# A one-column memset on VectorE replaced by a one-column tensor_tensor, 192 times, in an attention and mixture-of-experts kernel on one core

## The reference

```python
x = L0_attn_x                                   # (4, 512, 256)
xn = layernorm(x)
# attention: 16 query heads, 4 key/value heads, head size 128, rotary embedding with xpos scale
q, k, v = xn @ Wq, xn @ Wk, xn @ Wv
scores = einsum('bhqd,bhkd->bhqk', q, k) / sqrt(128)
attn = softmax(where(causal, scores, -inf))
s = (attn @ v) @ Wo
# feed-forward: 16 experts of 176, the best 2 of each token, and a shared expert of 352
g = silu(moe(xn) + shared(xn))
x = x + s * g
```

## Time and profile before

| | us |
|---|---|
| median of 3 runs | 763.02 |
| lowest, highest | 761.98, 763.47 |
| the profiled execution, its own time | 763.02 |
| its span, first to last instruction | 761.2 |

### The profile page before, as it was taken

One profiled execution on the slowest core, in us unless ns is written; L12 is line 12 of the kernel. 1 busy time (PEld: TensorE's weight loads), 2 busy tenths in 40 slices (PEclk: granted clock), 3 DMA queues, 4 the chain that ended last, 5 costly groups with the idle time before them and its releaser, 6 DMA issues.

```text
span 761.2 us, 17791 instructions
## 1 busy us (share of the span) xinstructions
PE 669.6 (88%) x5090; PEld 470.8 (62%) x5091; DVE 635.3 (83%) x1756; ACT 457.4 (60%) x1269; POOL 514.8 (68%) x543
## 2 busy tenths in 40 slices
PE   3678876789999999999999999999985879999983
PEld 1256544456667666676666766667664558778751
DVE  6988999988999899998999989999875975454477
ACT  3684645446756567575675766757664756666642
POOL 4676656648678886888868888688844734444474
PEclk9999999989999999999999999999998999999997
DMA  9490000500000000000000000000004864444562
GB/s 297 158 318 19 1 1 0 135 23 15 1 14 7 7 14 0 14 7 7 14 0 14 14 0 14 0 14 14 0 15 131 233 102 131 124 132 133 194 249 83
DMA packets 45747, 50.40 MB, mean 66 GB/s; under 512 B 9906, under 2 KB 39058, under 8 KB 45714
## 3 DMA queue, kind: packets, MB, share of 16 engines
q1 hardware_dynamic: 41602, 39.44, 17.6%
q0 software_dynamic: 3840, 10.52, 3.9%
q10 hardware_dynamic: 272, 0.02, 0.0%
HBM read 31.01 MB, written 18.96 MB: 66 GB/s over the span
## 4 chain that ended last, share of the span: by engine, by line
POOL 36%; DVE 21%; issue 19%; PE 15%; ACT 5%; DMA 3%; POOLq 0%; SPq 0%; DVEq 0%; ACTq 0%
POOL arena L520 15%; POOL arena L507 9%; POOL arena L514 8%; PE bank L1455 6%; PE bank L1495 5%; POOL xs_dram L537 4%; DVE arena L375 3%; ACT arena L660 2%; DVE arena L1026 2%; PE bank L1464 2%; DMA arena<-x 1%; DVE arena L1000 1%; DVE arena L1001 1%; DVE s_sb L1174 1%; PE bank L1475 1%
## 5 line engine op out<-in xcount | busy, mean ns | idle before, releaser
L520 POOL TENSOR_TENSOR arena<-arena,rinv 128x128 f32<-128x128 f32 (+3 forms) x256 | 176.4, 720 | 119.4 <-DVE rinv L1020 119.4
L660 ACT ACTIVATE arena<-bank,nmax 128x512 f32<-128x512 f32 (+3 forms) x256 | 132.5, 533 | 69.8 <-DVE nmax L1014 69.8
L1014 DVE CUSTOM_DVE_ANT_0 bank<-bank,mask_b 128x512 f32<-128x512 f32 (+3 forms) x256 | 118.1, 516 | 11.9 <-issue 11.9
L1328 PE MATMUL bank<-arena 128*128 128x512 f16 (+7 forms) x768 | 119.6, 307 | 3.4 <-DVE arena L1032 3.2
L1268 PE MATMUL bank<-xnT_hi,arena 128*128 (+1 forms) x320 | 111.0, 389 | 11.2 <-DVE arena L1001 6.2
L1299 PE MATMUL bank<-arena 128*128 128x512 f16 (+7 forms) x768 | 116.9, 303 | 3.2 <-POOL arena L514 3.1
L668 ACT CAST arena<-bank 128x512 f16<-128x512 f32 (+1 forms) x192 | 93.2, 522 | 42.0 <-PE bank L1312 40.4
L1312 PE MATMUL bank<-ident_f,arena 128*128 128x128 f32 x640 | 92.6, 276 | 25.0 <-DVE arena L1026 18.3
L1026 DVE TENSOR_TENSOR arena<-bank,arena 128x512 bf16<-128x512 f32 (+1 forms) x192 | 109.0, 596 | 3.0 <-ACT arena L668 0.9
L507 POOL TENSOR_TENSOR arena<-arena 128x512 f32<-128x512 f32 x77 | 99.7, 1295 | 7.1 <-DVE arena L1001 6.8
L1312 PEld LDWEIGHTS bank<-ident_f,arena 128*128 128x128 f32 x640 | 74.0, 142 | 37.8 <-DVE arena L1026 22.4
(11 more groups left out here) (147 smaller groups left out, 1259.8 us busy)
## 6 DMA issues: line engine op xcount, KB each, us to landing
xs_dram<-s_sb SPq DMA_DIRECT2D x4, 1548.0 KB, 14.3
arena<-xs_dram SPq DMA_DIRECT2D x48, 128.0 KB
stage<-w_gate_up SPq DMA_DIRECT2D x16, 352.0 KB
arena<-ys_dram SPq DMA_DIRECT2D x8, 512.0 KB, 6.6
stage<-w_down SPq DMA_DIRECT2D x16, 176.0 KB
stage<-wq SPq DMA_DIRECT2D x4, 512.0 KB, 8.7
stage<-wo SPq DMA_DIRECT2D x4, 512.0 KB, 7.3
stage<-x SPq DMA_DIRECT2D x1, 2048.0 KB
```

The costliest lines, as they stand in the source:

```text
L520: ins = pool.tensor_tensor(pr, pr, rinv[:, par, qt:qt + 1].to_broadcast([P, (qt + 1) * P]), ALU.mult)
L660: ins = act.activation(probs[par][:, P_AT[qt]:P_AT[qt] + n], score_bank[u][:, col:col + n], ACT.Exp, scale=-1.0, bias=nmax[:, par, qt:qt + ...
L1014: ins = dve.tensor_tensor_reduce(score_bank[u][:, col:col + n], score_bank[u][:, col:col + n], mask_b[:, S - n:S], -1.0, 3e38, ALU.add, AL ...
L1328: ins = pe.matmul(o_bank[:, kt * P:S], v_s[a][:, kt * DH:(kt + 1) * DH], pT[j % 2][m][:, PT_AT[kt]:PT_AT[kt] + n_q], start=(kt == 0 and n ...
```

## The change

A tile `one` of one float32 column is added, and POOL sets it to 1.0 once, behind its first memset. In `row_max` the memset of one column of `waited` becomes a tensor_tensor that multiplies `one` by `one` into the same column. It carries the same wait and stands at the same place, three times for each head. Since the new memset raises `zeroed` too, the counts that are waited for go up by one, and DVE waits for it once, before the first `row_max`. No other instruction is added, removed or moved on any engine.

```diff
+        one = sb("one", [P, 1], F32)
...
             pool.memset(s_sb[:], 0.0).then_inc(zeroed, 1)
+            pool.memset(one[:], 1.0).then_inc(zeroed, 1)
             pool.memset(ones_b[:], 1.0).then_inc(zeroed, 1)
...
                     dve.wait_ge(scores, h * 3 + u + 1)
-                    dve.memset(waited[:, par, u:u + 1], 0.0)
+                    dve.tensor_tensor(waited[:, par, u:u + 1], one[:], one[:], ALU.mult)
                     for qt, col in unit:
...
             dve.wait_ge(mask_zero, 1)
+            dve.wait_ge(zeroed, 2)
             row_max(0, 0)
...
-            dve.wait_ge(zeroed, 3)
+            dve.wait_ge(zeroed, 4)
...
-                pe.wait_ge(zeroed, 2)
+                pe.wait_ge(zeroed, 3)
```

## The result

| | before | after |
|---|---|---|
| median, us | 762.87 | 798.02 |
| lowest, highest | 761.98, 763.47 | 794.78, 802.08 |
| span of the profiled execution | 761.2 | 794.4 |

The ratio is 1.045, with a 95% interval of 1.0418 to 1.0482: 35 us slower, where +58 was forecast. First the page's busy line, to be read beside the earlier trace rows, then the stretch of the earlier trace rows.

What follows compares the result with a forecast made beforehand. PE bounds the loop at 31.0 us a round; with the waits DVE becomes the bound at 35.1. +43 us in 12 loop rounds and +15 elsewhere, +58 on 763.0, gives 821 us, range 788 to 859.

Steps and rivals of the forecast that it cites:

- The mechanism: In `row_max`, the two-SBUF-input instruction waits for the end of POOL's tensor_tensor in flight; 86%, centre 821 us.
- rivals 1 and 2: At the changed instruction: first, no blocking, 771 us, 8%; second, not slower, hidden like the memset, 763 us, 5%.
- the signs: Rows of `waited` up to 1.3 us, mean 0.5 to 0.6; loop round 35 us; DVE over 93%, PE under 92%.
- Rival 3: POOL's instructions are delayed by DVE as well: at most 0.1 us each, 12 a round; chance included in the 86%.
- The mean wait: Per changed instruction in the loop, arriving at a random moment of POOL's work: 0.37 us, thinned to 0.33.
- The instruction itself: Each changed instruction's own fixed cost on DVE's queue, without waiting: 0.08 us.
- Together: Wait plus own cost on DVE per loop round: 12 x (0.33 + 0.08) = 4.9 us more, giving 33.9 us.
- The idle time that is kept: In a loop round DVE keeps half of its 2.5 us idle time, 1.2 us, making the round 35.1 us.
- Outside the loop: The 48 instructions in prologue and rounds 0, 1, 2 and 15: 48 x 0.41 x 0.75 = +15 us.
- The lower bound: Waits line up within a head, 0.25 us each plus 0.04: +1.0 to +2.2 us a round, 789 to 803 us.
- that DVE waits for one POOL instruction only: A blocked DVE instruction waits only for the POOL instruction in flight and gets through before the next queued one.
- The clock: PE, less busy at 88%, might get 0.9 of its clock, 34.4 us a round: nothing added, reason for upper half.

Runs made afterwards that it cites:

- e1: Changed kernel with the one-column tensor_tensor replaced by a one-column reciprocal of `one` (one SBUF input instead of two): 766.73 us.
- e2: Changed kernel with the tensor_tensor reading two different one-column tiles instead of the same tile twice: 795.41 us.
- e8: Changed kernel with the tensor_tensor only ahead of the first unit of each head, memsets ahead of the other two: 790.85 us.
- e9: Changed kernel with a memset ahead of the first unit of each head, tensor_tensors ahead of the second and third: 769.78 us.
- e7: Changed kernel with two one-column tensor_tensors in each place, the second into a tile of its own: 811.29 us.
- e11: Changed kernel with the tensor_tensor replaced by a tensor_copy, `one` and the target two columns wide: 795.80 us.

## Why the prediction came out as it did

**The mechanism was right.** The wide spread of the rows, their ends with POOL's, DVE as the bound of the loop, the unchanged end: all as written. One input less takes nearly all of the loss away (e1), and the same tile twice makes no difference (e2), so rivals 1 and 2 fall. What the Trainium skill, page "SBUF — State Buffer", section "Who interferes with whom", infers of descriptor generation, which I gave 5 us, holds as well: the row at 391.97 passes beside an indirect DMA. Four of the signs had the right direction and the wrong size: the mean row is 0.38 us for 0.5 to 0.6, the longest 2.04 for 1.3, the round 33.6 for 35, and PE is busy 93% where under 92% was said.

**Rival 3 had shown itself in one row before.** POOL's 1.44 us at 140.43 followed a DVE instruction of 256 columns and two SBUF inputs:

```profile
138.44 2.30 DVE L953 TENSOR_TENSOR compare<-held,steps 128x256 f32<-128x256 f32 x1
```

It ends at 140.74, POOL's instruction ahead at 140.46, and the next one is 0.17 us longer than the usual 1.27. With one column nothing of the kind is left (446.9 and 446.7 us of POOL's tensor_tensors, before and after).

**The size was too large, 58 for 35 us.** Per loop round I had +3.6 us and it was +2.1. By the steps of the sum:

- *The mean wait* was put at 0.33 us, for an instruction that comes at a random moment. It measures 2.8/12 = 0.23. This is the largest error, 1.2 us per round. The moments are not random. The 12 places fall at the same phase of POOL's work in each round, and 6 of 12 pass without a wait. Over the whole execution 102 of the 192 instructions start while a POOL tensor_tensor is in flight, 53%, where I had 74%. They also make their own gaps: POOL's division waits for DVE's reciprocal, which comes later now, so POOL stands idle more. The wait for it was 57.2 us in the earlier trace rows; in the same stretch after:

```profile
POOL arena L522 <- DVE rinv L1022: 72.3, 26, 3.8
```

- *The instruction itself* was put at 0.08 us, 1.0 per round, all of it arriving. Its start-to-start time is 0.07, but the run with one input shows that only 0.14 us per round arrives. Part of it is hidden, and the memset it replaces was not free: I had read it so because the steps were 0.13 us for 128 columns with or without it. Behind the tensor_tensor the custom instruction of 384 columns holds the queue 0.48 us and the one of 256 columns 0.34, where it was 0.51 and 0.38 behind a memset:

```profile
384.26 0.55 DVE L1016 CUSTOM_DVE_ANT_0 bank<-bank,mask_b 128x384 f32<-128x384 f32 x1
...
384.74 0.32 DVE L1016 CUSTOM_DVE_ANT_0 bank<-bank,mask_b 128x128 f32<-128x128 f32 x1
...
385.06 0.42 DVE L1016 CUSTOM_DVE_ANT_0 bank<-bank,mask_b 128x256 f32<-128x256 f32 x1
385.40 0.13 DVE L1016 DVE_READ_ACCUMULATOR2_ANT nmax<- 128x1 f32 x1
```

- *Together* DVE's busy time was to grow by 4.9 us a round. It grew by 3.0 (270.47 us in 283.70, or 8.44 rounds, is 32.0 a round, for 29.0).
- *The idle time that is kept* was 1.2 us of 2.5; it is 33.6 - 32.0 = 1.6. That was sized well enough, but its working (a half) had no ground. That it came near is luck; e8 and e9 show what it depends on: what stands before the first unit arrives nearly in full, what stands before the others is partly covered.
- *Outside the loop* I had +15 us for 48 places; it is 8 in the profiled executions (33 less 25), and 10 by the medians. The mean wait of these 48 is 0.24 us, for 0.33.
- *The lower bound* had the better sizes: with 0.25 us for each wait and 0.04 for the instruction it gave 1.0 to 2.2 us a round and 789 to 803 us. Measured are 0.23, 2.1 and 798. Its reason, that later instructions of a head come about 0.7 us behind a POOL boundary, holds for one head of the four, where they come 0.5 and 0.65 us behind one (408.47 to 409.01, 409.59 to 410.24 in the rows above).

**Stated too firmly:** that DVE waits for one POOL instruction only. So it is in 87 of the 88 long rows, but at 179.94 us it did not get in at the boundary. DVE's row, and POOL's two:

```profile
179.94 2.04 DVE L1013 TENSOR_TENSOR waited<-one 128x1 f32<-128x1 f32 x1
```
```profile
179.58 1.16 POOL L516 TENSOR_TENSOR arena<-arena 128x512 bf16<-128x512 f32 x1
180.71 1.25 POOL L509 TENSOR_TENSOR arena<-arena 128x512 f32<-128x512 f32 x1
```

It ends with the second (181.98 beside 181.96). The like occurs once each in e2, e7, e8 and e11 (2.03 to 2.04 us), and in e9 at 175.95 (1.42 us). Why the boundary at 180.7 was missed is not known.

**The clock.** I had feared that PE, less busy, would be granted less. In the loop it was busy 93% and granted 1.00, so that reason for the upper half fell there. Before the loop it did not quite: in the stretch that had 0.98 before the granted clock is now 0.86.

```profile
96.00:135.00 39.00, 29.41 (x197) 19.22 (x196) 36.42 (x81) 16.10 (x43) 24.98 (x25) 0.86 0.00 1
```

DVE is the fuller engine there (36.42 of 39 us), and how much of the 8 us outside the loop the clock makes no run tells.

No version beats the kernel before. None leaves the memset out altogether: a custom instruction that carries the wait for `scores` itself was not tried.

## What to carry to other kernels

In this kernel a VectorE tensor_tensor that reads two operands from SBUF waits for the end of whatever GpSimd tensor_tensor is in flight, however small it is itself (0.15 us alone, 2.8 us of waiting in 12 of them), and a copy of two columns does the same. So where both engines are busy, keep one operand in PSUM (677 to 693 ns in all 80 cases of the earlier trace rows), or use a form that did not wait here: a one-column memset, reciprocal or copy, or a reduction. Count such instructions by how many there are and by the length of GpSimd's instructions, not by their own columns. And when an engine with some idle time gets longer, ask for each place whether its idle time lies behind it in the same chain: here the same kind of wait cost nearly all of its time ahead of the first unit, and about a third ahead of the others.

## What the runs showed of the hardware that was not expected

- A float32 copy of one column (96 to 155 ns) never waits for GpSimd, one of two columns does (up to 2.04 us; the kernel with it takes 30 us longer).
- A second one-column memset ahead of a custom instruction costs about 0.09 us per round of 12, under 0.01 us each; a one-column reciprocal or copy in place of the first 0.14 us per round.
- A tensor_tensor of one column waited up to 2.04 us, through two GpSimd instructions in a row, in one place of the program. The GpSimd instructions that it waited for were not longer for it.
